# Performer context of eight sequences: values of a head stationary, its key features moving, in four column groups, and a turn at the end

## The reference, cut to what matters

```python
qp = softmax_kernel(q, proj, is_query=True)      # b, h, n, 64
kp = softmax_kernel(k, proj, is_query=False)     # ratio * (exp(xp - diag - stab) + 1e-4)
k_sum = jnp.sum(kp, axis=2)
denom = jnp.einsum('bhnm,bhm->bhn', qp, k_sum)
ctx = jnp.einsum('bhnm,bhnd->bhmd', kp, v)
out = jnp.einsum('bhnm,bhmd->bhnd', qp, ctx) / denom[..., None]
```

## Time and profile before

| what | us |
|---|---|
| median of 3 runs | 2827.17 (2812.53, 2828.0, 2827.17) |
| span of the profiled execution | 2816.7 |
| PE busy, PEld busy | 2497.9, 2270.6 |
| DVE, ACT, POOL busy | 2077.3, 1248.8, 865.1 |
| context matmuls, weight loads busy (L1606) | 120.1 |
| Performer attention, from the first tail to the last | 1145 to 1860 |

### The profile page before, as it was taken

The page is one execution under the profiler, slowest core; times in us unless marked ns, Lnnn a source line. Parts: engine busy times, 40 slices in busy tenths (PEclk is TensorE's granted clock), DMA queues, the critical chain, the costliest instruction groups (busy, mean ns, idle before and its releaser), DMA issues. The chain is left out here.

```text
span 2816.7 us, 44565 instructions
## 1 busy us (share of the span) xinstructions
PE 2497.9 (89%) x16076; PEld 2270.6 (81%) x16076; DVE 2077.3 (74%) x3623; ACT 1248.8 (44%) x1992; POOL 865.1 (31%) x517
## 2 busy tenths in 40 slices
PE   7999996788888886999999999994988889699999
PEld 6888885778877885889888988883887778599998
DVE  5666666999999996655665566547899998766664
ACT  4444443444434432544554565432433334344444
POOL 1111112656665652320232023204334433211110
PEclk9999997998999997999999999976999999899999
DMA  5000000000000000000000000002000010000000
GB/s 162 0 0 0 0 0 18 1 1 0 0 0 0 0 1 15 1 15 15 7 7 15 11 7 11 15 12 68 16 23 15 15 45 0 32 24 23 22 22 30
DMA packets 43119, 45.99 MB, mean 16 GB/s; under 512 B 2977, under 2 KB 42017, under 8 KB 42785
## 3 DMA queue, kind: packets, MB, share of 16 engines
q1 hardware_dynamic: 43040, 44.95, 5.0%
HBM read 28.16 MB, written 16.78 MB: 16 GB/s over the span
## 5 line engine op out<-in xcount | busy, mean ns | idle before, releaser
L1745 ACT ACTIVATE m_a<-m_ps_wide,m_b 128x512 f32<-128x512 f32 x128 | 88.3, 690 | 286.4 <-PE m_ps_wide L277 201.1
L1713 PE MATMUL m_ps_z<-m_w_hi,m_a_hi 128*128 128x256 f32 x512 | 152.7, 298 | 52.8 <-DVE m_a_lo L1785 52.8
L275 PE MATMUL f_ps_down<-f_down_w_hi,f_h_T_hi 128*128 128x256 f32 (+1 forms) x384 | 132.9, 346 | 68.1 <-DVE f_h_T_lo L932 68.1
L1745 ACT ACTIVATE d_a<-d_ps_wide,d_b 128x512 f32<-128x512 f32 x128 | 88.3, 690 | 190.5 <-PE d_ps_wide L277 190.4
L1785 DVE TENSOR_TENSOR d_a_lo<-d_a,d_a_hi 128x512 fp32r<-128x512 f32 x128 | 86.7, 689 | 111.8 <-ACT d_a_hi L1749 111.4
L1237 POOL TENSOR_TENSOR p_kf<-p_kf,p_k_shift 128x1024 f32<-128x1024 f32 x64 | 119.4, 1902 | 155.5 <-DVE p_k_shift L1371 155.5
L1713 PEld LDWEIGHTS m_ps_z<-m_w_hi,m_a_hi 128*128 128x128 f32 x512 | 103.2, 202 | 67.0 <-DVE m_a_lo L1785 62.0
L187 ACT ACTIVATE f_h_magic<-f_h_magic,minus_magic 128x1408 f32<-128x1408 f32 x32 | 47.1, 1473 | 240.7 <-DVE f_h_magic L183 240.7
L275 PEld LDWEIGHTS f_ps_down<-f_down_w_hi,f_h_T_hi 128*128 128x128 f32 (+1 forms) x384 | 84.8, 221 | 84.3 <-DVE f_h_T_lo L932 74.2
L1713 PE MATMUL m_ps_z<-m_w_lo,m_a_hi 128*128 128x256 f32 x512 | 149.9, 293 | 0.0
L1713 PE MATMUL m_ps_z<-m_w_hi,m_a_lo 128*128 128x256 f32 x512 | 149.8, 293 | 0.0
(11 more groups left out here) (342 smaller groups left out, 9081.5 us busy)
## 6 DMA issues: line engine op xcount, KB each, us to landing
residual<-in_x SPq DMA_DIRECT2D x8, 1024.0 KB, 11.8
attn<-p_attn SPq DMA_DIRECT2D x32, 256.0 KB, 2.1
m_attn<-attn SPq DMA_DIRECT2D x16, 512.0 KB, 3.9
out<-residual SPq DMA_DIRECT2D x16, 512.0 KB, 2.9
raw_weights<-in_d_q SPq DMA_DIRECT2D x2, 1024.0 KB, 7.2
d_scale<-in_d_scale SPq DMA_DIRECT2D x2, 1024.0 KB, 5.9
raw_weights<-in_m_w1T SPq DMA_DIRECT2D x1, 1024.0 KB, 5.1
raw_weights<-in_m_w2T SPq DMA_DIRECT2D x1, 1024.0 KB, 9.7
```

Of the source, the lines that this page charges most:

```text
L275: pe.matmul(out, lhsT[0], rhs[0], start=start, stop=False)
L1713: mm = pe.matmul(z, a, w[:, f, :], start=(f == 0 and k == 0 and j % 2 == 0), stop=(f == FC - 1 and k == 2), skip_group_check=True)
L1745: act.activation(self.a[f % RING][:, :], self.ps_wide[f % 2][:, :], self.func, bias=self.b1[:, f:f + 1])
```

## The change

The operands of the context product are swapped. For each of 16 heads the 17 columns of values and one are stationary, and the 64 key features of the head move. The result is 17 x 64 and stands on partitions 32j to 32j + 16 of `ps_a`, where j = 0 to 3 is one of four groups of 32 columns of the array; four heads share a group, at different columns of the bank (`ctx_at`). `column_order` lets heads follow one another in different groups; the two records of one fp32 matmul lie in the same group. In the compiled program these matmuls have a tile of 128 x 32 at column 0, 32, 64 or 96, all others around them one of 128 x 128. The matmul with `v_sum` becomes 16 in the same way, with 64 columns of `keps` moving.

The sum then has features along the columns, and the output product needs them on the partitions: DVE copies 128 x 256 from `ps_a` to `ctxT` (which lies in `squares`), PE turns it in two transposes into `ps_b`, and the two DVE copies into `ctx_pair` read `ps_b`. One fp32 matmul with zeros (272 columns) is done once, at the start, so that all of `ps_a` is defined.

```diff
+        ctxT = squares[:, 0, 0, 0:KD * P]
...
                 dve.wait_ge(ctx_done, b + 1)
+                dve.tensor_copy(ctxT[:, :], ps_a[:, 0:KD * P]).then_inc(ctxT_copied, 1)
+                dve.wait_ge(ctx_turned, b + 1)
                 for r in range(2):
                     rows = slice(r * M, (r + 1) * M)
                     dve.tensor_copy(ctx_pair[rows, :, r * VW:(r + 1) * VW],
-                                    ps_a[rows, 0:PAIRS * 2 * VW].rearrange("p (k w) -> p k w", k=PAIRS)
-                                    [:, :, r * VW:(r + 1) * VW]).then_inc(ctx_copied, 1)
+                                    ps_b[rows, 0:KD * P].rearrange("p (k w) -> p k w", k=PAIRS)
+                                    [:, :, 0:VW]).then_inc(ctx_copied, 1)
...
+            def column_order():
+                return [HC * c + 2 * j + r for c in range(KD) for r in range(2) for j in range(CT)]
+
+            def ctx_at(h):
+                j, at = h % HC // 2, (h // HC * 2 + h % 2) * M
+                return ps_a[j * VP:j * VP + VW, at:at + M]
...
                             pe.wait_ge(v_summed, (b + 1) * (TB - 1))
-                            pe.matmul(ps_a[:, 0:HEADS * VW], keps[:, :], v_sum[:, :], start=True, stop=False,
-                                      skip_group_check=True)
-                        vt = v[:, j].rearrange("p h w -> p (h w)")
-                        for k in range(PAIRS):
-                            mm = pe.matmul(ps_a[:, k * 2 * VW:(k + 1) * 2 * VW], kf[:, j, k * P:(k + 1) * P],
-                                           vt[:, k * 2 * VW:(k + 1) * 2 * VW], start=False, stop=(j == TB - 1),
-                                           skip_group_check=True)
+                            for h in column_order():
+                                pe.matmul(ctx_at(h), v_sum[:, h, :], keps[:, 0:M], start=(h < HC and h % 2 == 0), stop=False,
+                                          skip_group_check=True)
+                        for h in column_order():
+                            mm = pe.matmul(ctx_at(h), v[:, j, h, :], kf[:, j, h * M:(h + 1) * M], start=False,
+                                           stop=(j == TB - 1), skip_group_check=True)
                         if j == TB - 1:
                             mm.then_inc(ctx_done, 1)
+                pe.wait_ge(ctxT_copied, b + 1)
+                for c in range(KD):
+                    mm = pe.transpose(ps_b[:, c * P:(c + 1) * P], ctxT[:, c * P:(c + 1) * P], ident[:, :])
+                mm.then_inc(ctx_turned, 1)
```

More of the change, by code:

```diff
@@ L1046 @@
 HC = HEADS // KD
+VP = 32
+CT = P // VP
 class PerformerRaw:
@@ L1156, in performer_attention @@
         v = sbuf("p_v", [P, TB, HEADS, VW])
-        v_sum = sbuf("p_v_sum", [P, HEADS * VW])
+        v_sum = sbuf("p_v_sum", [P, HEADS, VW])
         halfsq_k, halfsq_q = (sbuf(f"p_halfsq_{e}", [P, TB, HEADS]) for e in "kq")
@@ L1194, in performer_attention @@
         k_shifted, k_exp = sem("p_k_shifted"), sem("p_k_exp")
-        ctx_done, ctx_copied = sem("p_ctx_done"), sem("p_ctx_copied")
+        ctx_done, ctxT_copied = sem("p_ctx_done"), sem("p_ctxT_copied")
+        ctx_turned, ctx_copied = sem("p_ctx_turned"), sem("p_ctx_copied")
         qf_done, q_shifted, q_exp = sem("p_qf_done"), sem("p_q_shifted"), sem("p_q_exp")
@@ L1220, in tile_of_v @@
             def tile_of_v(i):
-                return v[:, i].rearrange("p h w -> p (h w)")
+                return v[:, i, :, :]
             with pool.Fori(0, B) as b:
@@ L1230, in _ @@
                         pool.wait_ge(v_summed, b * (TB - 1) + i - 1)
-                    pool.tensor_tensor(v_sum[:, :], v_sum[:, :] if i > 1 else tile_of_v(0), tile_of_v(i),
-                                       ALU.add).then_inc(v_summed, 1)
+                    so_far = v_sum[:, :, :]
+                    pool.tensor_tensor(so_far, so_far if i > 1 else tile_of_v(0), tile_of_v(i), ALU.add).then_inc(v_summed, 1)
                 pool.wait_ge(k_shift_ready, b + 1)
@@ L1601, in tail @@
                             pe.wait_ge(v_summed, (b + 1) * (TB - 1))
-                            pe.matmul(ps_a[:, 0:HEADS * VW], keps[:, :], v_sum[:, :], start=True, stop=False,
-                                      skip_group_check=True)
-                        vt = v[:, j].rearrange("p h w -> p (h w)")
-                        for k in range(PAIRS):
-                            mm = pe.matmul(ps_a[:, k * 2 * VW:(k + 1) * 2 * VW], kf[:, j, k * P:(k + 1) * P],
-                                           vt[:, k * 2 * VW:(k + 1) * 2 * VW], start=False, stop=(j == TB - 1),
-                                           skip_group_check=True)
+                            for h in column_order():
[4 more added lines that the diff above has]
+                                           stop=(j == TB - 1), skip_group_check=True)
                         if j == TB - 1:
                             mm.then_inc(ctx_done, 1)
+                pe.wait_ge(ctxT_copied, b + 1)
+                for c in range(KD):
+                    mm = pe.transpose(ps_b[:, c * P:(c + 1) * P], ctxT[:, c * P:(c + 1) * P], ident[:, :])
+                mm.then_inc(ctx_turned, 1)
             pe.wait_ge(ones_set, 2)
+            pe.matmul(ps_a[:, 0:PAIRS * 2 * VW], ident[:, :], ctx_pair[:, :, :].rearrange("p k w -> p (k w)"),
+                      start=True, stop=True)
             run(tail, merged)(pe)
```

## The result

| | before | after |
|---|---|---|
| median of 4 runs each, us | 2820.18 (2812.53 to 2828.0) | 2845.85 (2843.6 to 2851.41) |
| span of the profiled execution, us | 2816.7 | 2843.0 |
| mean granted clock in it | 0.938 | 0.925 |

The changed kernel takes 1.0103 times as long, with an interval of 1.0071 to 1.0135. The forecast was no change, 2813 us. The time lies inside the stated range of 2800 to 2872, but the kernel became slower and not a little faster.

What follows compares the result with a forecast made beforehand. PE was taken to bound the rounds by only 0.39 us over DVE; -10.5 (first seven tails), -3.0 (last tail) and -0.5 sum to -14 us, subtracted from the median: 2813 us, range 2800 to 2872.

Steps and rivals of the forecast that it cites:

- C: New length of a context block on PE, 1.71 us before, taken as 1.1 with the column groups working at once.
- the 0.03 that I gave as the sign: Context records about 0.03 us apart on average, with a block near 1.1 us, would show the block length right.
- The rule that I weighed: Changing tile mode drains TensorE; at 0.14 us twice a context block, the block takes 1.24 to 1.38, sum -12 to -5.
- the 0.14 that I took: Allowance in us per context block on PE for going to narrow tiles and back.
- (a): Context blocks: groups not at once, or records one in about 0.06 us; block 1.86, +29, 2856 us; chance 0.21.
- (b): Context blocks: records as far apart as before; block 3.58 us, +153, 2980 us; chance 0.10.
- the ceiling: Rounds of the first seven tails can give back only DVE's waits, 10.5 us, whatever the context costs.
- -10.5: Rounds of the first seven tails: DVE's waits go, in us.
- -3.0: Rounds of the last tail: PE's shorter blocks come in full, since DVE waits 5.9 us there.
- The end of a tail: Last reduction to output product: 5.84 us against 5.90, the shorter blocks paying for the turn.
- (c): Narrow records lower the granted clock for a stretch each tail, 3 us lost each; +24, 2837 us; chance 0.08.
- The signs of being wrong: Block over 1.45 us, ACT's exponentials later, or first to last reduction still 26 us with DVE idle in it.

Runs made afterwards that it cites:

- short wide blocks: Kernel before with three of the eight pairs of heads in each context block, tiles still wide, no turn: 2853.91 us, ratio 1.0117.
- turn alone: Kernel before plus only the 128 x 256 copy, the two transposes and the wait between them, context product unchanged: 2851.73 us, ratio 1.0128.
- filled twice: Changed kernel plus unused 512-column matmuls, six ahead of the transposes of tile 6 and three behind the turn: 2814.98 us, ratio 0.9979.
- group by group: Changed kernel with another order of heads, all four of one column group and then those of the next: 2835.54 us, ratio 1.0066.

## Why the prediction was wrong

**The context block: too dear.** I took C = 1.1, it is 0.69, since I let the two records of one head follow each other with only the next head's first beside the second. In the trace records wait only within their group: four records in 0.056 us. Records lie 0.018 us apart on average, not the 0.03 that I gave as the sign. The rule that I weighed, that changing the mode drains TensorE (the Trainium skill, "TensorEngine Tiling (Array Packing)", Tiling Modes), agrees with the trace in kind: 0.12 us going in, and 0.15 from the last record's start to the features coming out, of which 0.056 is the record's own. The two add up to 0.21 beyond the records, between the 0.14 that I took and the 0.28 of the rule. Rivals (a) and (b) are refuted. The 62 ns a matmul that the Trainium skill, "TensorE: Matmul & The Clock Gate", Back-to-back issue gap, gives for decoding in software, the trace does not bear out for these records, at 0.018 us.

**The rounds: right in kind, the ceiling a little low.** Forecast -10.5 and -3.0, measured -11.5 (185.2 to 173.7 us in the first seven tails) and -3.8 (26.34 to 22.52). The waits are gone in the first seven, and DVE is the bound there. But the agreement is closer than the working deserves. The last four of the seven intervals between reductions, all at clock 1.00, became 12.9 us shorter over these tails, though DVE's 25 waits in them held only the 10.5 of the forecast: with each wait some 0.1 us more went (a late round is 3.57, forecast 3.66). The second and third intervals lost 1.0 in sum. Against that the first interval of each tail took 2.4 us more in sum, and 14.9 us of these first intervals ran at the lower clock in place of 7.8.

**The end of a tail: the first wrong step.** "The last transposes need the exponential, which ends at ... 3.78, so they start at 3.85." The exponential does end at 3.78. But they need `ps_turn` too, and ACT's queue has the copy that frees it behind that exponential: they start at 4.83, and at full clock the product at 6.83 in place of 5.84. Before, in the second tail, the same copy was finished 4.7 after the reduction and PE came to the transposes at 5.0, so nothing showed the wait. The buffer stood in my own description of the kernel. At full clock this costs 0.93 us in each of eight tails, 7.4 of the 10.3 measured. Of the other 2.9, four ends in which the clock fell hold 2.7, and the longer end of the eighth tail 0.2.

**The clock: the step that decided.** I had it as rival (c), with a chance of 0.08 and a price of 3 us a tail, and argued against it that "the features and transposes stand between the blocks, and PE with 34 moving columns in these blocks kept 1.00". Both are true of rounds 2 to 7, where the clock is 1.00 after the change as well. The reason was looked for in the wrong place. Behind round 7 there are no features, and there the change takes 1.0 us out of each of two blocks while ACT's chain, which releases the transposes, is no shorter. So the end has PE busy for 3.2 of 6.8 us. I had worked out the start times of this end and had not read the gap between them as a risk to the clock. The cause in (c), narrow records, is not borne out either: short wide blocks lose more, so narrow records aren't needed, and the same narrow blocks lose nothing in merged once 512-column matmuls stand in the waits, so they aren't enough. The price was +30.0 in merged and 2.7 in the ends.

So -15.4 + 7.4 + 30.0 + 2.9 + 1.3 = +26.2 us at the profiled execution, and the medians differ by 25.7. With the turn moved and the waits filled, which keeps the clock, the forecast's terms come out (0.9948).

That the time lies between 2800 and 2872 is luck: the upper end was set by rival (a), slow records, which the trace refutes, and the loss came from elsewhere. The signs of being wrong didn't catch it: C is under 1.45, the exponentials come on time, and the clock is 1.00 in rounds 2 to 7. Of the signs only the product, at 6.83 in place of 5.8 to 5.9, told that something was off, and none looked at the clock behind round 7.

What stays open: how much idle the clock bears. The turn alone, with 0.7 us, is hit in 3 of 7; filled twice, with 1.3 us, in 0 of 7; group by group, with 1.2 us, in 4 of 7, though PE is busy there for 5.69 us of the end and for 5.50 when filled twice. So idle time alone doesn't order these kernels. What the rest of the end consists of (512 moving columns or 34 and 64), where the idle lies, or when it comes may count too, and no run here separates these.

## What to carry to other kernels

Before you shorten work on PE, whose clock fell here for want of work, list what that work covered: draw the new start times of the stretch and look at the idle time they leave, not only at the end of the chain. For each start in the new schedule name all semaphores it waits for, buffers included, even those whose waits were zero before. A shortened stretch is worth its time only if what releases the next one gets shorter too; where it doesn't, put independent work there, and even work without use can pay (0.9979 against 1.0056 for 0.7 us of it a tail).

## What the runs showed of the hardware

- fp32 matmuls (two records each) in four groups of 32 columns run at once: 32 records with 64 moving columns in 0.57 us, four in 0.056 us. One group after the other they take 1.27, and even then, by the spacing of the starts (0.236 and 0.242), the next group's first record stands beside the fifth of the group before, so PE had begun it with three records of the other group still to come.
- The granted clock fell with PE idle for as little as 0.7 us ahead of the output product (turn alone, three of seven sequences), and stayed down for 10.2 us in which PE was busy throughout. The Trainium skill, "TensorE: Matmul & The Clock Gate", A second HAM failure mode: psum-queue depth-cycling, tells of short idles between groups of matmuls that make the clock swing; the trace agrees in kind, with merged stretches of 58.05 us in place of 53.33 in that kernel.
- The stretch behind a hit is as dense as before it fell, 15.00 us busy of 15.00, and shows the loss only in its count of records, 83 in place of 117: the busy share alone hides it.
